# First two layers: spills of q and k issued together, six score banks for the first thirteen pairs

## What is computed

```python
q = rope(x @ Wq); k = rope(x @ Wk); v = x @ Wv
scores = einsum('bhqd,bhkd->bhqk', q, k) * scale   # layer 0: causal mask
out = einsum('bhqk,bhkd->bhqd', softmax(scores), v) @ Wo
```

## Time and profile before

| | |
|---|---|
| median of 3 runs | 3225.08 us (3224.71 to 3231.12) |
| profiled execution, its own time | 3228.11 us |
| its span, first to last instruction | 3226.8 us |
| mean granted clock of TensorE | 0.966 |
| busy over the span: PE, DVE, ACT, POOL | 2926.5, 2524.8, 2207.4, 2008.9 us |
| attention of layers 0 and 1 | scores from 52.86 to about 656 us |
| time from 60 to 80 us | PE busy 14.90, DVE 12.38, clock 0.50 |
| time from 200 to 300 us (layer 0) | PE busy 97.52, DVE 83.05, clock 1.00 |
| time from 500 to 600 us (layer 1) | PE busy 82.77, DVE 78.10, clock 0.91 |

### The profile page before, as it was taken

One profiled execution on the slowest core, in us unless ns is written; L12 is line 12 of the kernel. 1 busy time (PEld: TensorE's weight loads), 2 busy tenths in 40 slices (PEclk: granted clock), 3 DMA queues, 4 the chain that ended last, 5 costly groups with the idle time before them and its releaser, 6 DMA issues.

```text
span 3226.8 us, 72034 instructions
## 1 busy us (share of the span) xinstructions
PE 2926.5 (91%) x24662; PEld 2238.6 (69%) x24663; DVE 2524.8 (78%) x5836; ACT 2207.4 (68%) x6152; POOL 2008.9 (62%) x2045
## 2 busy tenths in 40 slices
PE   5999888897799989999979999999999999999997
PEld 4666554465688868787867777777777777777775
DVE  6788887757777765564568888888888888888886
ACT  4566655653355556456448888888888888888885
POOL 2633333232455555335148888888888888888884
PEclk7999989998899989999989999999999999999998
DMA  3222422100000010201000000000000000000000
GB/s 110 74 77 77 128 78 76 52 1 7 1 1 1 1 50 24 63 1 50 14 14 2 2 2 2 2 2 2 2 2 2 2 2 2 1 2 2 1 2 27
DMA packets 68872, 77.15 MB, mean 24 GB/s; under 512 B 8017, under 2 KB 60321, under 8 KB 68385
## 3 DMA queue, kind: packets, MB, share of 16 engines
q1 hardware_dynamic: 64912, 71.10, 7.2%
q10 hardware_dynamic: 3600, 1.46, 0.2%
HBM read 52.61 MB, written 18.87 MB: 22 GB/s over the span
## 4 chain that ended last, share of the span: by engine, by line
PE 38%; DVE 9%; POOL 8%; issue 5%; ACT 4%; DVEq 0%; POOLq 0%; ACTq 0%
PE psum L2556 9%; PE psum L2538 7%; PE psum L2520 6%; POOL attn_p L3018 4%; DVE attn_pt L2817 2%; DVE sb_few L2804 2%; PE psum L1902 2%; PE psum L1753 2%; ACT attn_p L2662 2%; PE psum L1995 2%; PE psum L1755 2%; PE psum L1754 2%; PE psum L2583 2%; PE psum L1802 2%; PE psum L2462 1%
## 5 line engine op out<-in xcount | busy, mean ns | idle before, releaser
L3018 POOL TENSOR_TENSOR attn_p<-attn_p,sb_few 128x512 f32<-128x512 f32 x768 | 796.0, 1050 | 174.8 <-DVE sb_few L2811 173.5
L2662 ACT ACTIVATE attn_p<-psum,sb_few 128x256 f32<-128x256 f32 x1536 | 720.2, 479 | 61.4 <-DVE sb_few L2804 61.3
L2804 DVE TENSOR_REDUCE sb_few<-psum 128x2 f32<-128x512 f32 x768 | 507.9, 679 | 12.7 <-PE psum L2520 7.0
L2538 PE MATMUL psum<-sb_kept,attn_p 128*128 128x128 f32 x3072 | 411.4, 277 | 33.2 <-DVE attn_pt L2817 29.4
L2556 PE MATMUL psum<-attn_pt,attn_v 128*64 128x256 f32 x3072 | 384.2, 387 | 30.7 <-DVE attn_pt L2817 30.7
L502 DVE TENSOR_REDUCE sb_a_nm<-psum 128x2 f32<-128x512 f32 x512 | 329.0, 684 | 87.5 <-PE psum L392 54.1
L2538 PEld LDWEIGHTS psum<-sb_kept,attn_p 128*128 128x128 f32 x3072 | 335.4, 141 | 82.5 <-issue 30.7
L568 ACT ACTIVATE sb_a_pt<-psum 128x512 f32<-128x512 f32 x512 | 278.5, 597 | 100.4 <-PE psum L399 69.7
L2662 ACT ACTIVATION_READ_ACCUMULATOR attn_p<-psum,sb_few 128x1 f32 x1536 | 319.6, 208 | 0.0
L2556 PEld LDWEIGHTS psum<-attn_pt,attn_v 128*64 128x64 f32 x3072 | 202.7, 136 | 157.0 <-issue 75.5
L2817 DVE COPY attn_pt<-psum 128x512 f32<-128x512 f32 x384 | 263.7, 687 | 34.0 <-PE psum L2538 28.7
(11 more groups left out here) (441 smaller groups left out, 7752.1 us busy)
## 6 DMA issues: line engine op xcount, KB each, us to landing
sb_a_spread<-a_spilled SPq DMA_DIRECT2D x64, 256.0 KB, 2.9
a_spilled<-sb_a_part_hi SPq DMA_DIRECT2D x64, 128.0 KB
a_spilled<-sb_a_part_lo SPq DMA_DIRECT2D x64, 128.0 KB
sb_a_spread<-a_spilled SPq DMA_DIRECT2D x64, 128.0 KB, 2.7
sb_gate_up<-in_L_ffn_Wg SPq DMA_DIRECT2D x32, 128.0 KB
sb_gate_up<-in_L_ffn_Wu SPq DMA_DIRECT2D x32, 128.0 KB
sb_down_w<-in_L_ffn_Wd SPq DMA_DIRECT2D x32, 128.0 KB, 2.5
sb_x<-in_L_attn_x SPq DMA_DIRECT2D x4, 512.0 KB, 7.3
```

Of the source, the lines that this page charges most:

```text
L2538: mm = pe.transpose(PT(e)[:, kt * N + t * P:kt * N + (t + 1) * P], Pr[p % 3][:, e, t, kt * P:(kt + 1) * P], c.ident)
L2662: ins = act.activation(Pr[p % 3][:, e, t, :], S(p, e)[:, t * N:(t + 1) * N], ACT.Exp, bias=nm[:, p % 4, e, t:t + 1], accum_out=rsum[:, p % ...
L2804: dve.tensor_reduce(nm[:, p % 4, e, :], S(p, e).rearrange("p (t n) -> p t n", t=TB), AX.X, ALU.max, negate=True).then_inc(maxed.sem, 1)
L3018: pool.tensor_tensor(P3, P3, spread(rinv[:, p % 4, e, :], N), ALU.mult).then_inc(normed[e].sem, 1)
```

## The change

First, `S` takes six banks in turn for pairs below 13, which in the opening are all free, and the waits follow: for p from 3 to 12 `scores(p)` waits for the second maximum of pair p - 3, where it waited for the first maximum of pair p - 1. `scores_by_key(0)`, the first user of banks 3 and 4 for keys, waits for the first maximum of pair 11. From p = 13 on the waits are as before. Second, the loop over q and k in SP's program is cut in two for every batch: first both spills with their waits for the parts, then for q and after it for k the wait for the spill, the wait for the landing buffer, and the load.

```diff
--- before.py
+++ after.py
@@ -254,7 +254,7 @@
     NB8 = len(layers) * B
     pe, act, dve, pool, sp = nc.tensor, nc.scalar, nc.vector, nc.gpsimd, nc.sync
     O, OT, M = c.banks[6][:, 0:N], c.banks[6][:, N:2 * N], c.banks[7]
-    S = lambda p, e: c.banks[(2 * p + e) % 3]
+    S = lambda p, e: c.banks[(2 * p + e) % (6 if p < AHEAD else 3)]
     ST = lambda p, e: c.banks[3 + (2 * p + e) % 3]
     GQ, ROW = GQ8, ROW8
     PB = H8 // 2
@@ -358,8 +358,10 @@
             if p == 0:
                 pe.wait_ge(*beside.scaled.all())
                 pe.wait_ge(*masks(0))
-            if p:
+            if p >= AHEAD:
                 pe.wait_ge(*maxed(2 * p - 2))
+            elif p >= 3:
+                pe.wait_ge(*maxed(2 * p - 5))
             causal = layer(b)[3]
             for t in range(TB):
                 for e in range(2):
@@ -376,6 +378,8 @@
                 pe.wait_ge(*maxima_laid(32 * (b + 1) - 1))
             if p:
                 pe.wait_ge(*exped(2 * p - 2))
+            else:
+                pe.wait_ge(*maxed(2 * AHEAD - 4))
             causal = layer(b)[3]
             for t in range(TB):
                 for e in range(2):
@@ -676,6 +680,8 @@
                 for n, half in enumerate((part_hi[j][:, b % 2, :], part_lo[j][:, b % 2, :])):
                     dst = bass.AP(tensor=box, offset=n * wide, ap=[[N, GQ], [2 * wide, ROW], [1, N]])
                     sp.dma_start(dst, half.bitcast(F32)).then_inc(away[j].sem, 16)
+            for j in range(2):
+                box = tiles.spilled[2 * j + b % 2]
                 sp.wait_ge(*away[j](32 * (b + 1) - 1))
                 if b:
                     sp.wait_ge(*laid(2 * (b - 1) + j))
```

## The result

The changed kernel takes **3181.3 us**, the median of 4 runs (3178.7 to 3188.0), against 3224.9 for the kernel before on the same chip: ratio **0.9864**, 95% interval 0.9844 to 0.9883. So it is faster by 1.4%, where 1.8% was forecast: 3168, in a range of 3152 to 3196. One run of a later kernel (rounding at step 6) was slow, 6811.9 us where its others took 3175 to 3179, and is left out of its median. The profiled execution has a span of 3180.4 us against 3226.8, 46.4 less, and a mean granted clock of 0.975 against 0.966.

What follows compares the result with a forecast made beforehand. Bounds: the opening's scores waiting for maxima, TensorE in layer 0, and layer 1's 18.46 us cycle of laying, spilling and loading k. Gains of 10 + 42 + 5 = 57 us from 3225.1 gave 3168, range 3152 to 3196.

Steps and rivals of the forecast that it cites:

- The opening: Scores of the first thirteen pairs over six banks, paced by VectorE's 1.29 us: 9.5 us less, 10 with the clock.
- The clock in the opening: Denser opening scores might bring 2.4 GHz, gaining about 2 us on projections and first batch pairs; 0.5 was taken.
- The first five intervals of layer 1: Between turns of the maxima, masks or layer 0's norm still add work: 18.2, 16.3, 16.1, then 15.8 each.
- The ten at 14.9: Ten later layer 1 intervals, set by TensorE's and VectorE's own work: 14.9 us each, 149.0 of 231.2; 42 us less.
- The shortened ring: Layer 1, laying k to laying the next k: parts 5.5, spill 5.3, load 3.7; 14.5 us instead of 18.46.
- rival A: Layer 1's cycle from laying k to the next stays the bound, at 15.7 to 16.5 us: about 3187; chance 0.16.
- The last two intervals: End of layer 1, without projections: 25.8 us for 32.6, 6.8 less; depending on the clock 0 to 7, 5 taken.
- q's load: Load behind k's spill in SP's order: 4.5 us instead of 3.7, still 0.8 ahead of need, changing nothing in the sum.
- rival B: q's load waits in full for k's spill, 9.0 us, making a 16.8 us cycle through q: 3196; chance 0.06.
- C: Only the opening gains, because something else of 17.7 us stands behind the k cycle in layer 1: 3215; chance 0.06.
- D: Slower: q's load takes 11.5 us, making batches of layers 0 and 1 19.3 us: 3246; chance 0.03.
- E: More than forecast: layer 1 batches at 14.3 us and the full gain of tail and clock: 3158; chance 0.13.

Runs made afterwards that it cites:

- rounding at step 6: Changed kernel with VectorE's ten rounding instructions for a later stage's ternary weights moved from step 3 to step 6 of a batch: 3175.7 us, 0.9835; repeated 3176.8, 0.9836.
- second execution: The changed kernel run once more, unaltered, beside later kernels on another chip: 3187.3 us, ratio 0.9868 to the kernel before.
- the kernel whose ring has slack: Changed kernel with rounding on GpSimd, plus each batch's high half spilled once cast, ahead of the low half: 3180.4 us, ratio 0.9844 to the kernel before.
- the rounding on GpSimd: Changed kernel with the ten rounding steps of the ternary weights done by GpSimd in place of VectorE: 3177.1 us, ratio 0.9833; repeated 3177.1, 0.9832.
- spills only: Changed kernel with the opening's six banks taken back to three, keeping SP's new spill order: 3189.5 us, ratio 0.9873 to the kernel before.
- twice the spill: Changed kernel with k's spill issued a second time, to DRAM space of its own, before q's load: 3202.6 us (one run).

## Why the prediction was right in sign and 13 us short

**The opening** (10 forecast, 6.8 and 9.5 measured in two executions). The mechanism is as forecast, and the pace is not quite: VectorE's 1.29 was to set it. In the first execution, at 1.2 GHz, TensorE's 1.26 does, and VectorE is level with it, busy without a gap from 52.69 to 60.00 (the 7.31 us of the table). So there the two rope turns that I charged to VectorE (2.4 in all) are not the price. TensorE's own projections are: 3.07 - 1.26 = 1.81 each, then 0.2 for L349 and 0.85 for the keys of pair 0. From first score to pair 13's it is 72.40 - 51.32 = 21.1, where 72.8 - 52.86 = 19.9 was forecast: a gain of 8.35 instead of 9.5. In the second execution the clock is up from 63.8 to 74, and there VectorE is the pace, as forecast: 72.65 - 53.23 = 19.4. The wait that the change added before the keys of pair 0, said to hold nothing up, then costs TensorE 1 us:
```profile
71.55 0.50 PE L387 MATMUL psum<-sb_a_q,sb_a_k 32*128 32x256 f32 x4 [0.99 <-DVE sb_a_nm L506]
```

The keys of pair 0, forecast near 72, came at 71.70 in the first execution, and batch 2's k was hidden.

**The clock in the opening** (0.5 forecast). It stays undecided from run to run, and that is 2 to 3 us: the first interval of L349 is 17.6 in the kernel after and 15.65 in its second execution.

**The first five intervals of layer 1** (82.2 forecast as 18.2, 16.3, 16.1, 15.8 and 15.8). Measured 18.18, 16.53, 16.75, 15.90, 14.78: 82.1. The sum is luck in part, since the third is 0.65 longer and the fifth 1.0 shorter than forecast.

**The ten at 14.9** (149.0 forecast, 156.3 measured, 15.63 each). Here is the term that was sized wrong, 7.3 of the 10.6 us that the profile is short of the forecast. The step behind it is 15.93 - 1.60 = 14.33 as TensorE's floor, raised to 14.9. It took the wait on GpSimd out whole, as if little stood behind it. The runs show three things that did:
- The rounding ahead of the settling. With it left out the ten intervals average 15.26, with it at step 6 15.48 and 15.38, on GpSimd 15.46 and 15.43; the changed kernel has 15.63 and 15.71 in its two executions. That is 0.15 to 0.45 less. VectorE's 14.21 of 15.93 were read as an amount of work with 1.72 to spare; what counted was one instruction, grown to 0.95 beside GpSimd, in front of an answer that TensorE was waiting for.
- The shortened ring, rival A, at 15.2 instead of the 14.5 of the sum, in the kernels where the rounding is out of the way. k's spill and load take 9.8 in the round shown, not 9.0. In the kernel after itself they take 8.4 to 9.6 from 446 us on, near the forecast, and A's signs are missing: GpSimd is idle before laying k for 0.8 to 2.1 us there instead of 5, and TensorE no longer waits for the laid k.
- Behind both, by the waits alone, ScalarE's exponentials: in the kernel whose ring has slack the interval is 15.23, of which TensorE is busy 13.9. In the kernel before, that wait was 3.4 us in 158, while TensorE waited elsewhere.

How the 0.7 us of an interval divide among the three is not shown, since each hides the next.

Besides, one batch of the ten ran at a clock of 0.90 and took 16.75, 1.15 more than its neighbour.

**The last two intervals** (5 forecast, 3.3 measured). The clock came up as hoped, 1.00 instead of 0.5 in part of them. The rounding goes with the rest: VectorE is busy 26.45 of 29.35 us, and with the rounding on GpSimd the two take 27.7, which is the forecast's 27.6. The split between these two intervals and the ones before depends on where a rounding falls: spills only has 28.0 with the rounding in place, after a long interval of 16.5.

**q's load** (0.8 later forecast, laid 4.5 after its issue; rival B 9.0). Measured 5.15, and 7.8 behind twice the spill. The row of k's spill behind q's load understated it. The Trainium skill's ring order (DMA: Bandwidth & Descriptors, Queues, rings and completion order) pointed the same way, and further. The delay is far from B's size: it costs layer 0 nothing (the milestones there are 18.18 apart), and in layer 1 it is no longer than the ring through k, since k is laid after it anyway.

**Rivals** C, D and E are out: layer 1 gained, no batch of layer 0 is longer, no run of the changed kernel came below 3178. The time lies above the 3160 to 3178 that the forecast itself was given (0.54), between it and A's 3187; the wide range covers it. The rest of the miss is 1.7 in the last intervals, 1.7 up to index 14, and 2.7 between the profiled executions and the medians.

## What to carry to other kernels

When a wait is taken off an engine, its length is not the gain: look for what else that engine would be waiting for at the same moment, above all single instructions that stand in another engine's order ahead of an answer, and run the batch once with each removed. A background instruction belongs behind the answers that others wait for, and where no other engine is busy beside it; the move of one line from step 3 to step 6 was worth 0.2 to 0.3% here, as much as leaving the work out. The best version of this study is the changed kernel with that move, or with the rounding on GpSimd: 3176 to 3177 us, ratio 0.983 to 0.984.

## What the hardware showed that I had not expected

The clock does not rise at a fixed time after TensorE becomes busy in the opening. In the kernel after TensorE is busy without a gap from 51.32 to past 71 us, and the granted clock is 0.50, 1.2 GHz, up to 81.6. In its second execution, with the same instructions, the clock rises at 63.8 and is 0.50 again from 74 to 80.8; TensorE was busy in 5.5 of the 8 us before that fall. The Trainium skill (TensorE: Matmul & The Clock Gate, Part 1) lets one expect a rise soon after dense work begins, and a small scatter of its moment. Here the early rise is missing, and the scatter between the two executions is 18 us. What makes it late is open.

The same VectorE instructions, the ten roundings, took 0.42 to 0.68 us with GpSimd idle and 0.94 to 1.23 when they started just behind one of GpSimd's. Why is not shown. GpSimd's L629 in turn took 1.05 at 480.95 beside such a rounding, where it takes 0.73 otherwise. In the kernel before, where the rounding met L622 and L624, it took 0.62 to 0.89.

A single batch in an otherwise steady stretch can fall to 0.90 (16.75 us among 15.60) and does so once in one execution and three times in another, at least, which alone makes some 1 to 4 us between profiled executions of kernels whose code there is the same.
